# First stage of an attention and mixture-of-experts block, rebuilt: scores and heads summed by transposes, centred weights, x in a ring

## What is computed

```python
x = x + attn(layernorm(x))          # first stage
x = x + experts(layernorm(x))       # second stage
# attn: q, k are 16 half heads of 16, v is 8 heads of 32, rotated by position
q, k = rotary(x @ Wq), rotary(x @ Wk); v = x @ Wv
# within ONE token: every head attends to the 8 heads of the same token
s1 = einsum('bsnd,bsmd->bsnm', q1, k1) / 16 ** 0.25        # and s2 with q2, k2
a = softmax(s1) @ v - lam * (softmax(s2) @ v)
a = a * rsqrt(mean(a * a, -1) + 1e-8) * ln_w + ln_b        # mean over each head's 32
attn = (a * (1 - LAMBDA_INIT)).reshape(b, s, 256) @ Wo
# experts: softmax gate over 8, the two best, up to 1024 rows per expert,
# silu(a) * g of 256 -> 768, then 384 -> 256, weighted sum of the two
```

## Time and profile before

| | |
|---|---|
| median of 3 runs | 835.03 us (834.35 to 835.39) |
| profiled execution, first to last instruction (span) | 831.7 us; its time with what lies around it was not recorded apart |
| instructions | 14035 |
| TensorE busy | 722.2 us (87%) |
| VectorE busy | 645.5 us (78%) |
| GpSimd busy | 635.8 us (76%) |
| ScalarE busy | 483.1 us (58%) |
| first score product, last score product start | 14.5 us, 544.2 us |
| first transposes of the second stage | 596.6 us |

### The profile page before, as it was taken

How to read it: one execution, slowest core, us unless ns; L and a number is a source line. 1 busy time by engine, 2 the same in 40 slices (tenths; PEclk the granted TensorE clock), 3 DMA queues, 4 the chain that set the end, 5 groups by cost and what they waited for, 6 DMA issues and landing times.

```text
span 831.7 us, 14035 instructions
## 1 busy us (share of the span) xinstructions
PE 722.2 (87%) x3552; PEld 564.1 (68%) x3552; DVE 645.5 (78%) x1549; ACT 483.1 (58%) x1969; POOL 635.8 (76%) x419
## 2 busy tenths in 40 slices
PE   5899989998988989898898988974299999999992
PEld 2577666666765666666666666653188898989882
DVE  4899999999998999998999999954045455545540
ACT  2567766666666667665776666744155455555541
POOL 2677799898897988989799898986546668656735
PEclk8999999999999999999999999996599999999996
DMA  6994100020120121010001001001234656465524
GB/s 202 347 341 150 52 33 33 28 91 28 39 78 30 38 77 40 26 60 29 4 1 51 1 1 51 1 1 51 67 102 71 148 121 147 74 146 139 75 26 50
DMA packets 57506, 63.41 MB, mean 76 GB/s; under 512 B 7113, under 2 KB 53294, under 8 KB 57440
## 3 DMA queue, kind: packets, MB, share of 16 engines
q1 hardware_dynamic: 42080, 45.66, 17.1%
q0 software_dynamic: 15360, 17.08, 11.7%
HBM read 27.57 MB, written 43.78 MB: 86 GB/s over the span
## 4 chain that ended last, share of the span: by engine, by line
DVE 53%; PE 28%; issue 10%; POOL 4%; ACT 1%; DMA 1%; SPq 1%; DVEq 1%; ACTq 0%; POOLq 0%
DVE s_raw L874 16%; DVE qk_prod L869 16%; PE bank_qk L801 8%; PE bank_wo L812 4%; PE bank_v L801 4%; PE bank_a L801 4%; PE bank_g L812 4%; DVE p_norm L899 2%; DVE s_sub L885 2%; DVE p_sum L890 2%; DVE bn L1052 2%; PE bank_t L792 2%; DVE x_all L861 2%; DVE p_rec L895 2%; POOL v_prod L404 1%
## 5 line engine op out<-in xcount | busy, mean ns | idle before, releaser
L404 POOL TENSOR_TENSOR v_prod<-w_att,v_sb 128x2048 f32<-128x2048 f32 x64 | 240.2, 3754 | 55.1 <-DVE w_att L906 47.8
L705 PE MATMUL bank_a<-v_prod,ident 128*128 128x256 f32 x768 | 184.0, 389 | 31.3 <-POOL v_prod L411 31.2
L705 PEld LDWEIGHTS bank_a<-v_prod,ident 128*128 128x128 f32 x768 | 141.8, 191 | 53.4 <-POOL v_prod L411 35.9
L438 POOL DMA_INDIRECT slot_table<-rows,g_slot x128 | 127.4, 995 | 33.5 <-issue 28.0
L480 POOL DMA_INDIRECT out_dram<-y_sb,e_tok x64 | 99.4, 1553 | 65.5 <-ACT y_sb L654 51.1
L869 DVE TENSOR_TENSOR qk_prod<-bank_qk,k_sb 128x2048 f32<-128x2048 f32 x64 | 145.9, 2280 | 0.5 <-issue 0.2
L874 DVE TENSOR_REDUCE s_raw<-qk_prod 128x128 f32<-128x2048 f32 x64 | 145.3, 2271 | 0.1
L693 PE MATMUL bank_qk<-wqkv,xT 128*128 128x512 f32 x256 | 129.6, 630 | 2.7 <-ACT xT L509 1.9
L532 ACT ACTIVATE a_sq<-a_sb 128x32 f32<-128x32 f32 x512 | 109.5, 222 | 0.0
L532 ACT ACTIVATION_READ_ACCUMULATOR a_sq<-a_sb 128x1 f32 x512 | 99.3, 194 | 0.0
L411 POOL TENSOR_TENSOR v_prod<-v_prod 128x512 f32<-128x512 f32 x64 | 81.0, 1265 | 5.0
(11 more groups left out here) (130 smaller groups left out, 1477.7 us busy)
## 6 DMA issues: line engine op xcount, KB each, us to landing
slot_table<-fill SPq DMA_DIRECT2D x8, 1056.0 KB, 13.3
xe<-slot_table SPq DMA_DIRECT2D x16, 528.0 KB, 3.7
out_dram<-x_all SPq DMA_DIRECT2D x8, 1024.0 KB, 4.6
x_all<-in_L_attn_x_dram SPq DMA_DIRECT2D x1, 6400.0 KB, 23.7
w<-in_L_ffn_c_fc_dram SPq DMA_DIRECT2D x8, 768.0 KB, 5.3
w<-in_L_ffn_c_proj_dram SPq DMA_DIRECT2D x8, 384.0 KB, 7.4
slot_table<-rows,g_slot POOLq DMA_INDIRECT x128, 2.4
x_all<-in_L_attn_x_dram SPq DMA_DIRECT2D x1, 1024.0 KB, 5.3
```

What stands on the lines that cost most here:

```text
L404: pool.tensor_tensor(v_prod[b][:, :, :, :], w_att[b][:, :, :].rearrange("p n m -> p m n").unsqueeze(3).to_broadcast([P, H, H, DV]), v_sb[b ...
L438: pool.indirect_dma_start(out=table, out_offset=bass.IndirectOffsetOnAxis(ap=g_slot[gb][:, j, k:k + 1], axis=0), in_=rows[:, r, :], in_off ...
L705: last = nc.tensor.matmul(bank_a[:, 0, :], ident[:, :], v_prod[b][:, m, :, :].rearrange("p n e -> p (n e)"), start=(m == 0), stop=(m == H ...
```

## The change

- **Weights are centred once.** TensorE takes the column means of Wq, Wk, Wv and the gate's weights, VectorE subtracts them (`centre_weights`). x is then transposed and projected raw. The factor 1/std of the first layer norm goes into the exponential's scale (squared, rstd_sq) and into the copy of v. The columns of Wq and Wk are written in another order, depth first.
- **Nine more columns** are in the projection of v and in that of the output: eight of the gate (its weights folded through Wo) and one with the negative mean. x in SBUF has these as columns 256 to 264, and `attention_added` updates them with x. The gate's transposes and matmuls go.
- **Scores:** VectorE still makes the 2048 products, laid out by depth. The sum over the depths is done by 16 transposes on TensorE that accumulate in bank_s (`sum_scores`). ScalarE copies the result, and one more transpose brings it back (`scores_to_tokens`).
- **Heads:** 16 transposes of 128 x 128 accumulate the eight products directly as the transposed a (`sum_heads`). GpSimd no longer folds.
- **Norm of a** in the transposed form: ScalarE squares 256 columns in one pass, TensorE averages per head with a block matrix (`mean_squares`), ScalarE takes logarithm and exponential, VectorE scales (`scale_a`). ln_b becomes a bias row, made once in nine VectorE passes (`bias_split`) and added by one bf16 matmul.
- **Layer norm statistics** come from two squares with an accumulator on ScalarE (`squares1`, `squares2`).
- **x is in a ring** of 16 tiles, loaded and stored in groups of four.
- The steps' orders and lags are new on each engine. The second stage keeps its instructions; two of its PSUM banks are others, and only GpSimd's first addition waits for the stored x.

```diff
--- before.py
+++ after.py
...
-                if live(i, 5):
-                    rms_scale(i - 5, (u - 5) % UNROLL, u)
-                if live(i, 13):
-                    past(pool, xn2_ready, i - 13)
-                    if u % GROUP == 1:
-                        row_waits(q - 3)
-                if live(i, 3):
-                    products(i - 3, (u - 3) % UNROLL)
-                if live(i, 13):
-                    scatter(i - 13, (u - 13) % UNROLL)
+                g, gb = group_step(i, u, q, SCATTER)
+                if g is not None:
+                    row_waits(g)
+                if live(i, 0):
+                    products(i, u % 2)
+                if live(i, SCATTER):
+                    scatter((u - SCATTER) % ROWS)
...
+            def copy_k(t, b):
+                past(act, qk_done, t)
                 past(act, qk_multiplied, t, 2)
-                nc.scalar.copy(k_sb[b][:, :], bank_qk[b][:, 1, :]).then_inc(k_copied, 1)
-                past(act, products_ready, t, 2)
-                nc.scalar.copy(v_sb[b][:, :], bank_v[:, 0, :]).then_inc(v_copied, 1)
-
-            def exp_scores(t, b):
+                nc.scalar.activation(k_sb[b][:, :], bank_qk[b][:, 1, :], ACT.Copy, scale=SCORE_SCALE).then_inc(k_copied, 1)
+
+            def copy_aux(t, u, g):
+                past(act, v_done, t)
+                past(act, glog_ready, g, RING // GROUP)
+                nc.scalar.copy(x_ring[:, u, E:E + AUX], bank_v[:, E:E + AUX]).then_inc(aux_copied, 1)
+
+            def squares1(t, u, s):
+                past(act, aux_copied, t)
+                nc.scalar.activation(sq_junk[:, 0, :], x_ring[:, u, 0:E], ACT.Square, bias=x_ring[:, u, E + NEXP:E + AUX],
+                                     accum_out=stat[:, s, 0:1]).then_inc(sq1_ready, 1)
+
+            def squares2(t, u, s):
+                past(act, x1_ready, t)
+                nc.scalar.activation(sq_junk[:, 1, :], x_ring[:, u, 0:E], ACT.Square, bias=x_ring[:, u, E + NEXP:E + AUX],
+                                     accum_out=stat[:, s, 1:2]).then_inc(sq2_ready, 1)
+
+            def roots(i, s):
+
+                if live(i, 1):
+                    past(act, sq1_ready, i - 1)
+                if live(i, 7):
+                    past(act, sq2_ready, i - 7)
+                nc.scalar.activation(stat_ln[:, s, :], stat[:, s, :], ACT.Ln, bias=eps_ln[:, :], scale=1.0 / E).then_inc(stat_log, 1)
+                past(act, stat_log, i - 1)
+                nc.scalar.activation(rstd_sq[:, s:s + 1], stat_ln[:, s, 0:1], ACT.Exp, scale=-1.0)
+                nc.scalar.activation(rstd[:, s, :], stat_ln[:, s, :], ACT.Exp, scale=-0.5).then_inc(rstd_ready, 1)
+
+            def copy_v(t, b, s):
+                past(act, rstd_ready, t)
+                past(act, multiplied, t, 2)
...
+            def exp_scores(t, b, s):
                 past(act, ssub_ready, t)
                 past(act, pnorm_ready, t, 2)
-                nc.scalar.activation(probs[b][:, :, :, :], s_sub[b][:, :, :, :], ACT.Exp, scale=SCORE_SCALE).then_inc(exp_done, 1)
...
+            def square_a(t, b):
                 past(act, a_summed, t)
+                past(act, ms_done, t, 2)
+                nc.scalar.activation(aT_sq[b][:, :], bank_a[b][:, 0:E], ACT.Square).then_inc(a_squared, 1)
+
+            def log_a(t, b):
+                past(act, ms_done, t)
+                nc.scalar.activation(aT_ln[b][:, :], bank_a[b][:, E:], ACT.Ln, bias=eps_rms[:, :], scale=1.0 / DV).then_inc(ms_log, 1)
+
...
+                nc.scalar.activation(aT_rms[b][:, :], aT_ln[b][:, :], ACT.Exp, scale=-0.5).then_inc(rms_ready, 1)
...
+            def normalise2(t, u, r, s):
+                past(act, rstd_ready, t + 6)
+                nc.scalar.activation(neg_mr[:, s:s + 1], x_ring[:, u, E + NEXP:E + AUX], ACT.Copy, scale=rstd[:, s, 1:2]).then_inc(neg_mr_ready, 1)
+                row_free(act, t, r)
+                past(act, neg_mr_ready, t)
+                nc.scalar.activation(rows[:, r, 0:E], x_ring[:, u, 0:E], ACT.Identity, bias=neg_mr[:, s:s + 1],
+                                     scale=rstd[:, s, 1:2]).then_inc(xn2_ready, 1)
...
+            def project_v(t, b):
...
+            def sum_scores(t, b):
+                past(pe, qk_multiplied, t)
+                past(pe, ssub_ready, t, 1)
+                for d in range(D):
+                    last = nc.tensor.matmul(bank_s[:, 0, :], qk_prod[b][:, d, :], ident[:, :], is_transpose=True,
+                                            start=(d == 0), stop=(d == D - 1), skip_group_check=True)
+                last.then_inc(sT_done, 1)
+
+            def scores_to_tokens(t, b):
+                past(pe, sT_copied, t)
+                nc.tensor.transpose(bank_s[:, 1, :], sT_sb[b][:, :], ident[:, :]).then_inc(scores_back, 1)
...
             def sum_heads(t, b):
-                past(pe, products_ready, t)
-                past(pe, a_copied, t, 1)
-                for m in range(H - FOLD):
-                    last = nc.tensor.matmul(bank_a[:, 0, :], ident[:, :],
-                                            v_prod[b][:, m, :, :].rearrange("p n e -> p (n e)"),
-                                            start=(m == 0), stop=(m == H - FOLD - 1))
+                past(pe, multiplied, t)
+                past(pe, an_ready, t, 2)
+                if isinstance(t, int) and t < 2:
+                    pe.wait_ge((woT_copied, gate_copied)[t], 1)
+                for m in range(H):
+                    for k in range(2):
+                        last = nc.tensor.matmul(bank_a[b][:, k * P:(k + 1) * P], v_prod[b][:, m, k * P:(k + 1) * P], ident[:, :],
+                                                is_transpose=True, start=(m == 0 and k == 0), stop=(m == H - 1), skip_group_check=True)
                 last.then_inc(a_summed, 1)
 
-            def transpose_a(t, b):
+            def mean_squares(t, b):
+                past(pe, a_squared, t)
+                nc.tensor.matmul(bank_a[b][:, E:], head_ones[:, :], aT_sq[b][:, :], start=True, stop=True).then_inc(ms_done, 1)
+
...
+                    nc.tensor.matmul(bank_wo[:, 0:E + AUX], aT_n[b][:, k * P:(k + 1) * P], wo_aug[:, k, :], start=(k == 0), stop=False)
+                nc.tensor.matmul(bank_wo[:, 0:E + AUX], ones[:, :], bias_parts[:, :], start=False, stop=True).then_inc(wo_done, 1)
...
+            POS = 15
+
             def step(i, u, q):
+                if live(i, 1):
+                    project_qk(i - 1, (u - 1) % 2)
+                if live(i, 2):
+                    sum_scores(i - 2, u % 2)
+                if live(i, 5):
+                    sum_heads(i - 5, (u - 5) % 2)
+                if live(i, 0):
+                    transpose_x(i, u, group_step(i, u, q, POS + 1)[0])
+                if isinstance(i, int) and i == 0:
+                    weight_means()
                 if live(i, 6):
-                    transpose_a(i - 6, (u - 6) % UNROLL)
-                if live(i, 8):
-                    transpose_x2(i - 8, (u - 8) % UNROLL)
-                if u % GROUP == 1 and group_live(q):
-                    positions(q - 3, (u // GROUP - 3) % 2)
+                    out_project(i - 6, u % 2)
+                if live(i, 5):
+                    mean_squares(i - 5, (u - 5) % 2)
+                if live(i, 1):
+                    project_v(i - 1, (u - 1) % 2)
+                if isinstance(i, int) and i == 1:
+                    transpose_wo()
+                if isinstance(i, int) and i == 2:
+                    fold_gate()
+                if isinstance(i, int) and i == 3:
+                    bias_row()
                 if live(i, 2):
-                    project(i - 2, (u - 2) % UNROLL)
-                if live(i, 6):
-                    out_project(i - 6, (u - 6) % UNROLL)
-                if live(i, 8):
-                    gate(i - 8, (u - 8) % UNROLL, q)
-                if live(i, 4):
-                    sum_heads(i - 4, (u - 4) % UNROLL)
-                if live(i, 1):
-                    transpose_x(i - 1, (u - 1) % UNROLL)
+                    scores_to_tokens(i - 2, u % 2)
+                g, gb = group_step(i, u, q, POS)
+                if g is not None:
+                    positions(g, gb, i)
 
             run_tiles(pe, step)
...
+                q4 = bank_qk[b][:, 0, :].rearrange("p (f n) -> p f n", n=H).unsqueeze(3).to_broadcast([P, 2 * D, H, H])
+                k4 = k_sb[b][:, :].rearrange("p (f m) -> p f m", m=H).unsqueeze(2).to_broadcast([P, 2 * D, H, H])
+                nc.vector.tensor_tensor(qk_prod[b][:, :, :].rearrange("p d (c n m) -> p (d c) n m", c=2, n=H), q4, k4,
+                                        ALU.mult).then_inc(qk_multiplied, 1)
 
...
+            def scale_a(t, b):
+                past(dve, rms_ready, t)
+                past(dve, wo_done, t, 2)
+                nc.vector.scalar_tensor_tensor(out=aT_n[b][:, :], in0=bank_a[b][:, 0:E], scalar=lnwb_s[:, 0:1], in1=aT_rms[b][:, :],
```

(5 more changed lines are left out.)

778 lines of the change are left out of this document (385 added, 393 removed).

## The result

The changed kernel takes 841.28 us (median of 4 runs, 839.84 to 844.90), the kernel before on the same chip 834.69: ratio 1.0086, 95% interval 1.0062 to 1.0111. A second timing in five rounds gave 840.91 against 834.90, 1.0075 (1.0049 to 1.0101). So it is slower by 0.8 to 0.9%, where 2% faster was forecast. The profiled execution has a span of 843.2 us and its time is 844.90; three others of the same program have spans of 838.1 to 840.4.

A forecast was written before the change was run, and what follows sets the result against it. VectorE bounds the first stage at 8.41 us per tile; TensorE would take over at 7.97 plus 0.1. 40 + 486 = 526 instead of 544.2, one us lost in the tail: span 815, forecast 818 us, range 805 to 830.

The forecast's parts named there:

- start of tile 3's product: Head of the first stage: tile 3's score product on VectorE starts at about 40 us, against 37.8 before.
- tile 3 to tile 63: First stage: 60 x (7.97 + 0.1) = 484, plus 5 for loop turns, less 3 for first steps: 486 us.
- last product to last scatter: Tail of the first stage on GpSimd: 47 us, against 46.2 before, so one us lost.
- experts, from the first transposes: Second stage, its instructions unchanged by the change: left at its 235 us.
- TensorE's step: TensorE's work per tile in the first stage: 7.97 us, up from 7.6, replacing VectorE's 8.41 as the bound.
- The allowance of 0.1 a tile for waits: First stage: 0.1 us added to TensorE's 7.97 us per tile for waits within a step.
- Every wait has 0.6 us or more to spare: TensorE's waits within a step, for the product, squares of a, v and score bank: all met with 0.6 us or more.
- two loop turns 2 x 2.6: Turns of the 16-tile loop: two at 2.6 us, 5 us in all, from VectorE's 2.58 us pause before.
- 8.5 us behind the last score product: Tail: GpSimd's last v_prod starts 8.5 us behind the last score product, from 552.71 - 544.2 in the old trace.
- rival 3: First stage: a ring of waits outlasts TensorE's step if ScalarE is 0.3 to 0.5 us late; 832 to 848 us; chance 0.14.
- The clock: Rival 1, TensorE's 34 transposes per step: granted clock drops, a step takes 10.6 us, about 975 us in all; chance 0.16.
- rival 2: TensorE's 35 transposes: weight loads set the spacing, at most 0.1275 us each, 0.7 us per tile more, 861 us; chance 0.10.

## Why the prediction was wrong

Its own sum, term by term, in spans (815 forecast, 843.2 measured in the profiled execution; a median execution has some 840):

| term | forecast | measured | miss |
|---|---|---|---|
| start of tile 3's product | 40 | 38.6 | -1.4 |
| tile 3 to tile 63 | 486 | 504.7 | +18.7 |
| last product to last scatter | 47 | 57.7 | +10.7 |
| experts, from the first transposes | 235 | 236.1 | +1 |

The second trace of the changed kernel has 501.0 and 56.1 in the second and third row, so these misses are good to some 4 and 2 us. No one step makes the whole miss: three terms were too small by some 10 us each, and together they turned a gain of 17 us into a loss.

- **TensorE's step was right.** 7.97 us forecast; 7.88 in plain tiles and 31.92 / 4 = 7.98 with the positions, wherever nothing else held it. The parts are right too, not only their sum: transposes 0.109 each against 0.107, the projection of v 0.89 against 0.89, the bias matmul 0.12 against 0.11. The allowance of 0.1 a tile for waits was not needed within a plain step (-5 us).
- **The failed step is "Every wait has 0.6 us or more to spare".** VectorE's passes were taken at the durations of the trace before, "four short passes", "with the work of a group at 8", and the list of waits leaves out the one that came: the output projection's for aT_n. In the new order v_prod starts right behind w_att, and the first pass behind it with two SBUF operands stands still until it ends, 3.8 us instead of 0.21. That reaches aT_n, and TensorE waits for it twice a group, 0.4 us each. In the old order v_prod ran beside qk_prod and s_raw, which do not stand still, so no row showed it in full. A smaller trace of it was there, beside the scatters: g_hot took 581 ns and w_att 473 where they take 208 and 275 (w_att of 416.64 took 0.52 us beside a scatter that ended at 417.03). It costs 32.9 - 31.9 = 1.0 us a group, some 12 us; removed, 11.5.
- **The loop's turn was taken over from a row that held for VectorE alone.** "two loop turns 2 x 2.6" = 5: measured 2 x 7.3, 9.4 us more (8.4 by the timing, 13.6 for two). 2.6 was the pause of the one engine that set the pace. With TensorE full and three others handing over to it every step, pauses of several engines count, one behind the other; this is read from the trace (the rows at 270.88, 280.69 and 283.74).
- **The tail: "8.5 us behind the last score product" was read from the old order.** Softmax of a tile now ends two VectorE steps behind its product. The v_prod of tile 61 starts 3.0 us behind the last product, and GpSimd, with two scatters between two v_prods, needs 6.2 us for each of the next two: 15.4. That is 7 us; the ring of 8 rows, a wait that the forecast did not have, is 2 to 4 (2.8 in the timing). The 2 x 14 scatters of 1.28 us were right.
- The table's rows and the 6 us between the last scatter and the first transposes make the forecast's 815. Of tile 3 to tile 63, +12, +9.4 and -5 make 16 of the 18.7; some 2 to 3 us are the first steps, for which I had taken 3 off. Two small slips beside: "on a slow clock" for the first projection is not in the rows, which have its 3.39 us only (the profile gives a granted clock of 1.00 from 8 to 12 us), and rival 3's upper end is 844 by its own numbers, 818 + 60 x 0.43.
- **The rivals.** The clock did not fall: it is 0.99 to 1.00, the 2.4 GHz level, from 100 to 540 us, with 34 transposes in a row in each step. The Trainium skill (TensorE: Matmul & The Clock Gate, Part 4: PE-mode transpose), by which it should have fallen, does not hold for this kernel; here transposes stand in a stream with other matmuls, and whether transposes alone keep the clock no run shows. The weight loads did not set the spacing (0.109 us a transpose, where rival 2 had 0.1275). Rival 3, a ring longer than TensorE's step, 832 to 848 us, has the time that came (841.28) in its range, and by luck: for its reason (hand-overs 0.3 to 0.5 us late on ScalarE in every step) the trace has nothing, plain steps have no such wait, and more than half of the loss lies in the turns and the tail. I gave it 0.14.

## What to carry to other kernels

When instructions move against each other, their durations are not constants. List for each VectorE pass which GpSimd instruction will run beside it, and put passes with two SBUF operands, and SBUF to SBUF passes of tensor_scalar's kind, where GpSimd is idle; moving only the longest hands the wait to the next of its kind, which is harmless only as long as what stands behind it is in time (3.43 us were, 3.8 were not). The price of a loop's turn, and of a drain at the end, is that of the order in which it was measured: where the bound moves to an engine that all others feed, count the pauses of all of them, and count the drain in the new order anew. The sum for an engine's own step can be exact, as here, and the forecast still wrong by 3%: the margin was 0.44 us a tile, 26 us in all, and standing still, turns and tail together took 27 to 33, by the two traces.

## What was not expected of the hardware

- A pass of 64 elements on VectorE takes from 0.21 to 3.80 us, by what GpSimd does beside it; one of 8 elements with a constant from 0.16 to 3.75. The other way round a GpSimd scatter went from 0.98 to 1.88 us beside an addition of 1.22.
- The turn of a loop of 16 tiles costs 6.8 us in the timing of one kernel (13.6 for two) and 1.4 us in that of another (2.8 for two), with the same loop.
- 34 transposes in a step of 7.88 us leave the granted clock at 1.00, at a spacing of 0.109 us.
